# Linear attention: two roundings and the low-rank scaling moved to ScalarE, the low-rank product split over two row groups

## The reference, cut to what matters

```python
def _L0_attn_ref(x, W_q, W_k, W_v, W_g, W_o, log_decay):   # chunks of 32 tokens
    Q = x @ W_q.T; K = x @ W_k.T; V = x @ W_v.T
    S = jnp.einsum('bncd,bnkd->bnck', Qc, Kc) * mask       # mask: decay ** distance, causal
    O = jnp.einsum('bnck,bnkd->bncd', S, Vc).reshape(B, T, D)
    gate = jax.nn.sigmoid(x @ W_g.T)
    return gate * O @ W_o.T + x
def _L0_ffn_ref(x, fast_b, w_fc, w_proj, u, v, gate):
    h = _bitlinear(x, w_fc) + gate * (x @ v.T @ fast_b.T @ u.T)
    r = jnp.maximum(h, 0.0)
    return _bitlinear(r * r, w_proj)
x = _layernorm(x + _L0_attn_ref(x, ...))
x = _layernorm(x + _L0_xattn_ref(x, ctx_1024, ...))
x = _layernorm(x + _L0_ffn_ref(x, ...))
```

## Time and profile before

| | |
|---|---|
| runs | 1279.95, 1280.46, 1281.04 us |
| median | 1280.46 us |
| the profiled execution's own time | 1279.73 us |
| its span in the trace | 1277.7 us |
| granted TensorE clock, mean | 0.999 of full speed |
| linear attention in the trace | from 0 to about 146 us on TensorE |
| PE, DVE, ACT, POOL busy | 98%, 72%, 62%, 60% of the span |

### The profile page before, as it was taken

The page is one execution under the profiler, slowest core; times in us unless marked ns, Lnnn a source line. Parts: engine busy times, 40 slices in busy tenths (PEclk is TensorE's granted clock), DMA queues, the critical chain, the costliest instruction groups (busy, mean ns, idle before and its releaser), DMA issues.

```text
span 1277.7 us, 21198 instructions
## 1 busy us (share of the span) xinstructions
PE 1256.6 (98%) x6900; PEld 844.6 (66%) x6900; DVE 922.2 (72%) x1816; ACT 794.0 (62%) x1061; POOL 768.3 (60%) x445
## 2 busy tenths in 40 slices
PE   8999999999999999999999999999999999999996
PEld 6887856666666666656665666657566655677775
DVE  6888877656775767477577756784766777778887
ACT  3444457655665656566656655574656676788885
POOL 2532368967876679487768767794877687100000
PEclk9999999999999999999999999999999999999999
DMA  6311220001100110010011001100200110021101
GB/s 221 116 67 50 69 66 18 4 1 34 37 2 17 33 19 0 17 50 2 0 33 35 0 17 33 19 0 17 50 2 0 34 18 17 14 70 50 49 17 50
DMA packets 99391, 43.08 MB, mean 34 GB/s; under 512 B 77168, under 2 KB 82048, under 8 KB 99344
## 3 DMA queue, kind: packets, MB, share of 16 engines
q1 hardware_dynamic: 98528, 39.33, 12.4%
q0 software_dynamic: 816, 3.15, 0.7%
HBM read 29.59 MB, written 12.58 MB: 33 GB/s over the span
## 4 chain that ended last, share of the span: by engine, by line
PE 92%; DVE 3%; POOL 2%; issue 1%; ACT 1%; DMA 1%; SPq 0%; POOLq 0%; DVEq 0%
PE ps L1400 17%; PE ps L1375 15%; PE ps L48 12%; PE ps L50 11%; PE ps L49 11%; PE ps L1391 4%; PE ps L1379 4%; PE ps L1436 2%; PE ps L1435 2%; PE ps L1437 2%; PE ps L1412 2%; PE ps L1829 2%; PE ps L1830 2%; PE ps L747 1%; PE ps L57 1%
## 5 line engine op out<-in xcount | busy, mean ns | idle before, releaser
L1200 DVE CUSTOM_DVE_ANT_0 junk<-ps,mask 128x512 bf16<-128x512 f32 x504 | 315.0, 687 | 87.7 <-PE ps L1391 86.3
L1066 ACT ACTIVATE prob<-ps,mcol 128x1024 f32<-128x1024 f32 x256 | 282.2, 1117 | 128.9 <-PE ps L1379 124.0
L981 POOL TENSOR_TENSOR acc<-acc,prob 128x1024 f32<-128x1024 f32 x126 | 300.6, 2385 | 11.5 <-POOL acc L981 0.4
L978 POOL TENSOR_TENSOR acc<-prob 128x1024 f32<-128x1024 f32 x63 | 150.6, 2391 | 193.9 <-ACT prob L1066 192.9
L1400 PE MATMUL ps<-prob,v_b 128*64 128x512 f32 x1024 | 244.5, 598 | 0.0
L995 POOL TENSOR_TENSOR acc_lo<-acc,acc_hi 128x1024 f16<-128x1024 f32 x63 | 136.5, 2167 | 5.1
L1400 PEld LDWEIGHTS ps<-prob,v_b 128*64 128x64 f32 x1024 | 67.8, 136 | 107.4 <-issue 73.7
L1375 PE MATMUL ps<-q_hi,k_hi 64*128 64x512 f32 x512 | 114.3, 442 | 1.8 <-issue 0.7
L1379 PE MATMUL ps<-shift,ones_r 64*128 64x512 f32 x512 | 101.8, 392 | 0.1
L1375 PE MATMUL ps<-q_hi,k_lo 64*128 64x512 f32 x512 | 101.4, 391 | 0.0
L1375 PE MATMUL ps<-q_lo,k_hi 64*128 64x512 f32 x512 | 101.4, 390 | 0.0
(11 more groups left out here) (265 smaller groups left out, 2927.6 us busy)
## 6 DMA issues: line engine op xcount, KB each, us to landing
shift<-nmx SPq DMA_DIRECT2D x512, 0.5 KB, 2.0
x_in<-in_xT SPq DMA_DIRECT2D x8, 512.0 KB, 3.7
x_scratch<-x_a SPq DMA_DIRECT2D x8, 512.0 KB, 2.9
raw<-in_cT SPq DMA_DIRECT2D x8, 512.0 KB, 3.7
raw<-x_scratch SPq DMA_DIRECT2D x8, 512.0 KB, 3.9
y<-x_scratch SPq DMA_DIRECT2D x8, 512.0 KB, 3.7
y_scratch<-y SPq DMA_DIRECT2D x8, 512.0 KB, 2.8
outT<-x SPq DMA_DIRECT2D x7, 512.0 KB, 2.8
```

The costliest lines, as they stand in the source:

```text
L978: pool.tensor_tensor(total, prob[:, 0], prob[:, 1], ALU.add).then_inc(acc_out, 1)
L981: pool.tensor_tensor(total, total, prob[:, kt], ALU.add).then_inc(acc_out, 1)
L1066: act.activation(prob[:, i].rearrange("p h t -> p (h t)"), SCORE[i % 2].rearrange("p h t -> p (h t)"), ACT.Exp, scale=SCALE, bias=mcol[:, ...
L1200: dve.tensor_tensor_reduce(junk[:, t % 2, h], SMAX[t % 2][:, h], mask[:], -1.0, -LOWEST, ALU.add, ALU.min, nmx[:, p % 2, t, h:h + 1]).then ...
```

## The change

- The rounding of `x` for batches 2 to 7 goes from VectorE to ScalarE: `round_x(b+1)` stands in step b between `deviation(b-2)` and `values(b)`; that of batch 2 stands ahead of `values(1)`. It waits for the load of `x`. VectorE waits for it ahead of the subtraction.
- The rounding of the gated product for batches 1 to 7 goes to ScalarE too: `round_gated(b)` behind `square(b-1)`.
- The low-rank scaling (`low_rank(0)` and `low_rank(1)`) goes to ScalarE behind `round_gated(3)` and `round_gated(4)`, and GpSimd's last instruction of each group waits for it.
- ScalarE's hardware loop over pairs of batches is written out; one load of the sigmoid table falls away by that (batch 2).
- `uT` and `mid` are held twice, in partitions 0 to 15 and 64 to 79, by a second DMA of `uT` and a second matmul and copy of `mid`. The two matmuls of `low_rank` take one row group each.

```diff
@@ linear_attention_phase @@
-    uT = sb(ctx, "uT", [RANK, HID], F32)
+    uT = sb(ctx, "uT", [P, HID], F32)
...
-    mid = sb(ctx, "mid", [RANK, D], F32)
+    mid = sb(ctx, "mid", [P, D], F32)
...
+    RANK_ROWS = (slice(0, RANK), slice(DH, DH + RANK))
@@ sync @@
-        sp.dma_start(uT[:], a["uT"]).then_inc(f_in, 16)
+        for rows in RANK_ROWS:
+            sp.dma_start(uT[rows], a["uT"]).then_inc(f_in, 16)
@@ gpsimd @@
             pool.wait_ge(f_step, n + 2)
+            pool.wait_ge(f_low, k + 1)
             pool.tensor_tensor(c["wfc"][:, k], c["wfc"][:, k], wfc[:, k], ALU.add).then_inc(f_step, 1)
@@ scalar @@
+        def round_x(b):
+            act.wait_ge(x_in[b % 2], 8 * (b - b % 2) + 16)
+            act.wait_ge(qm_ps, 2 * b - 2)
+            act.activation(x_hi[:, b % 2], x[:, b % 2], ACT.Copy).then_inc(x_rounded, 1)
+
+        def round_gated(b):
+            act.wait_ge(gate_used, b + 1)
+            act.wait_ge(y_ps, 2 * b)
+            act.activation(og_hi[:], og[:], ACT.Copy).then_inc(og_rounded, 1)
+
+        def low_rank(k):
+            act.wait_ge(f_low_ps, k + 1)
+            act.activation(c["wfc"][:, k, :], VY.rearrange("p a n -> p (a n)"), ACT.Identity,
+                           scale=gt[:, 0:1]).then_inc(f_low, 1)
...
-        act.wait_ge(f_in, 96)
+        act.wait_ge(f_in, 112)
...
+        round_x(2)
         values(1)
         square(0)
-        with act.Fori(2, B - 1, 2) as i:
-            for b in (i, i + 1):
-                front(b)
-                query_copies(b)
-                deviation(b - 2)
-                values(b)
-                square(b - 1)
+        round_gated(1)
+        for b in range(2, B):
+            front(b)
+            query_copies(b)
+            deviation(b - 2)
+            if b < B - 1:
+                round_x(b + 1)
+            values(b)
+            square(b - 1)
+            round_gated(b)
+            if b in (3, 4):
+                low_rank(b - 3)
@@ vector, split_x @@
-            if not (isinstance(b, int) and b < 2):
-                dve.wait_ge(qm_ps, 2 * b - 2)
-            dve.tensor_copy(x_hi[:, par], x[:, par]).then_inc(x_split, 1)
-            dve.wait_ge(x_split, 2 * b + 1)
...
+            if b < 2:
+                dve.tensor_copy(x_hi[:, par], x[:, par]).then_inc(x_split, 1)
+                dve.wait_ge(x_split, 2 * b + 1)
+            else:
+                dve.wait_ge(x_rounded, b - 1)
...
@@ vector, split_gated @@
-            dve.wait_ge(gate_used, b + 1)
-            if b > 0:
-                dve.wait_ge(y_ps, 2 * b)
-            dve.tensor_copy(og_hi[:], og[:]).then_inc(og_split, 1)
-            dve.wait_ge(og_split, 2 * b + 1)
...
+                dve.wait_ge(og_rounded, b)
...
-        def low_rank(k):
-            dve.wait_ge(f_low_ps, k + 1)
-            dve.tensor_scalar(c["wfc"][:, k, :], VY.rearrange("p a n -> p (a n)"), gt[:, 0:1], None,
-                              ALU.mult).then_inc(f_low, 1)
...
-        dve.tensor_copy(mid[:], ST[0:RANK, 0:D]).then_inc(f_mid, 1)
+        for rows in RANK_ROWS:
+            dve.tensor_copy(mid[rows], ST[rows, 0:D]).then_inc(f_mid, 1)
@@ tensor @@
-            pe.wait_ge(f_in, 96)
-            pe.matmul(ST[0:RANK, 0:D], bT[:], vr[:], start=True, stop=True).then_inc(f_mid_ps, 1)
+            pe.wait_ge(f_in, 112)
+            for rows in RANK_ROWS:
+                mm = pe.matmul(ST[rows, 0:D], bT[:], vr[:], start=True, stop=True)
+            mm.then_inc(f_mid_ps, 1)
...
-                mm = pe.matmul(VY[:, n], mid[:, k * P:(k + 1) * P], uT[:, n * T:(n + 1) * T], start=True, stop=True)
+                mm = pe.matmul(VY[:, n], mid[RANK_ROWS[n], k * P:(k + 1) * P], uT[RANK_ROWS[n], n * T:(n + 1) * T],
+                               start=True, stop=True)
```

More of the change, by code:

```diff
@@ L339, in linear_attention_phase @@
     f_above, f_below, f_step = sem("f_above"), sem("f_below"), sem("f_step")
+    x_rounded, og_rounded = sem("x_rounded"), sem("og_rounded")
     STAGED, CHUNKS = ("Wq", "Wk", "Wv"), 2 * DK
+    RANK_ROWS = (slice(0, RANK), slice(DH, DH + RANK))
     QO, G, VY, S, ST = ps[:, 0:2, :], ps[:, 2:4, :], ps[:, 4:6, :], ps[:, 6, :], ps[:, 7, :]
@@ L498, in split_x @@
             dve.wait_ge(x_in[par], 8 * (b - par) + 16)
-            if not (isinstance(b, int) and b < 2):
-                dve.wait_ge(qm_ps, 2 * b - 2)
-            dve.tensor_copy(x_hi[:, par], x[:, par]).then_inc(x_split, 1)
-            dve.wait_ge(x_split, 2 * b + 1)
-            dve.tensor_tensor(x_lo[:, par], x[:, par], f32(x_hi[:, par]), ALU.subtract).then_inc(x_split, 1)
+            if b < 2:
[3 more added lines that the diff above has]
+                dve.wait_ge(x_rounded, b - 1)
+            dve.tensor_tensor(x_lo[:, par], x[:, par], f32(x_hi[:, par]), ALU.subtract).then_inc(
+                x_split, 1 if b < 2 else 2)
         def split_weight(i, w, src):
@@ L594, in split_gated @@
         def split_gated(b):
-            dve.wait_ge(gate_used, b + 1)
-            if b > 0:
-                dve.wait_ge(y_ps, 2 * b)
-            dve.tensor_copy(og_hi[:], og[:]).then_inc(og_split, 1)
-            dve.wait_ge(og_split, 2 * b + 1)
-            dve.tensor_tensor(og_lo[:], og[:], f32(og_hi[:]), ALU.subtract).then_inc(og_split, 1)
+            if b == 0:
+                dve.wait_ge(gate_used, 1)
+                dve.tensor_copy(og_hi[:], og[:]).then_inc(og_split, 1)
+                dve.wait_ge(og_split, 1)
+            else:
+                dve.wait_ge(og_rounded, b)
+            dve.tensor_tensor(og_lo[:], og[:], f32(og_hi[:]), ALU.subtract).then_inc(og_split, 1 if b == 0 else 2)
         def scales():
@@ L648, in step @@
             if b in (3, 4):
-                low_rank(b - 3)
-            if b in (3, 4):
                 compare_in(b - 3)
@@ L784, in step @@
             if b == 1:
-                pe.wait_ge(f_mid, 1)
+                pe.wait_ge(f_mid, 2)
             mean(b - 1)
```

## The result

| | before | after |
|---|---|---|
| median of 5 runs each, run side by side | 1280.49 us (1279.95 to 1282.57) | 1287.77 us (1283.67 to 1288.09) |
| ratio, 95% interval | | 1.0040 (1.0026 to 1.0055) |
| the profiled execution | 1279.73 us, span 1277.7 | 1283.67 us, span 1281.7 |
| ACT, DVE, POOL busy | 62%, 72%, 60% | 63%, 71%, 60% |

The change makes the kernel slower by 0.4%. Measured again, 12 runs beside 35, the same pair gave 1284.73 against 1280.26 us, a ratio of 1.0041 (1.0021 to 1.0061), so the loss is about 4.5 us there. The time after lies above the predicted range, 1278.6 to 1283.3 us.

The account below looks back on a forecast made before the run. The prediction took TensorE, with 92% of the span, as the bound. Its terms, 0.2 + 3.25 - 2.0 - 0.95 = +0.5 us, made 1279.7 into 1280.2; median forecast 1281.0 us, range 1278.6 to 1283.3.

Parts of the forecast that it names:

- What bounds the kernel: Whole kernel: 92% of the span lies on TensorE, so only its own stream or its waits pay.
- The start, +0.2: Start, at middle: second uT load and second small matmul cost about 0.1 us each; bounds 0 and 0.7.
- Rounding of x, +3.25: Linear attention, steps 1, 2, 3, 4 and 6: attend waits 0.65 us each for ScalarE's rounding and value copy.
- Low-rank product, -2.0: Steps 3 and 4: two fp32 matmuls in two row groups take 0.91 us, not 1.91; 1.0 saved, twice.
- Rival B: Low-rank matmul pairs run one after the other, no overlap: +2.0 us, 1283.0; chance 0.10.
- Gated product and scaling at nothing: Linear attention: moving both to ScalarE costs nothing by itself; outputs and scores still find their inputs ready.
- Step 5, -0.95: Step 5: TensorE's stalls from VectorE held by GpSimd at tile_sum shrink from 2.5 to 1.55 us; bounds 0 and -1.85.
- Chances: Whole kernel: forecast 0.70; against a 0.2% difference, faster by more 0.09, slower by more 0.15, within 0.76.
- C: Rival: ScalarE takes x's landing later than thought, 1.1 us a step in place of 0.65: 1284.2 us; chance 0.11.
- The sum: Whole kernel: +0.5 us, made in linear attention and passed on whole; median forecast 1281.0 us.
- W: Theory of the experiments, not the prediction's: x's rounding stands ahead of the value copies, and attend waits for it.

Follow-up runs that it names:

- half of `x` ahead: Kernel before with only x's rounding on ScalarE, 512 columns ahead of the value copies, the rest between them: 1284.35 against 1281.19 us, ratio 1.0024.
- all ahead: Kernel before with only x's rounding moved to ScalarE, ahead of both value copies: 1285.60 against 1280.95 us, ratio 1.0033.
- between: Kernel before with only x's rounding moved to ScalarE, between the two value copies: 1280.30 us, ratio 0.9990.
- with `x` between and the late load: Changed kernel, x rounded between value copies, second uT load behind other weights: 1278.97 against 1280.95 us with three GpSimd waits, 1277.68 against 1281.19 without.
- GpSimd giving way: Changed kernel with three GpSimd waits until tile_sum of that step is done: 1281.53 against 1280.95 us, ratio 1.0003.
- the best kernel: Changed kernel, x rounded between value copies, second uT load behind all other weights, no GpSimd waits: 1277.68 against 1281.19 us, ratio 0.9974.

## Why the prediction was wrong, point by point

- **What bounds the kernel: right.** All but the +0.53 us at the start is waits on TensorE in linear attention, less the saving of the pairs, and what was passed on whole arrived nearly so (+3.7 us at `variance(6)`, +4.0 in the span).
- **The start, +0.2: nothing in this trace, above its bound in others.** From `attend(0)` to `middle` it is 1.99 us (1.98 before), and the second small matmul costs nothing (22.89 - 22.36 = 0.53 us, 0.54 before). The +0.53 ahead of `attend(0)` isn't this term: VectorE waited for the load of `WgT_l` until 7.35 us (6.71 before), and the loads of `uT` are issued only from 12.01. In the profiles of the other kernels `attend(0)` starts anywhere from 19.95 to 22.66 us. In four of the six traces with the second load early `middle` waited 0.86 to 1.04 us for the gate's load, more than the 0.7 of the bound; without it none of eight did.
- **Rounding of x, +3.25: right, and slightly low.** Issue to `attend` was forecast at 5.25 us and measured 5.26, 5.47, 5.45 and 5.39 in steps 1, 2, 3 and 6. Steps 1 to 3 lost 0.68, 0.80 and 0.89 in place of 0.65. In step 4 the wait was covered by the one at `mean`; I had counted it there.
- **Low-rank product, -2.0: right in kind, 15% too large.** The pair takes 1.06 us, so 0.85 is saved, twice: -1.7. Rival B (no overlap) fell.
- **Gated product and scaling at nothing: right for ScalarE, wrong for the rest.** ScalarE reaches the query copies later and no `scores` waits. Timeline of ScalarE, changed kernel, the scaling and what follows it:

```profile
78.90 1.10 ACT L485 ACTIVATE wfc<-ps,gt 128x1024 f32<-128x1024 f32 x1
80.02 1.28 ACT L440 ACT_TABLE_LOAD   x1
81.32 1.03 ACT L440 ACTIVATE gate<-ps 128x1024 f32<-128x1024 f32 x1
```

  0.02 us lies on either side of the table load: the drain that the Trainium skill, "ScalarE: Activation LUTs" (What ACT_TABLE_LOAD costs), adds isn't seen here. But the scaling left VectorE, and the comparison and GpSimd's three instructions behind it moved. Step 4 of the kernel before, VectorE and GpSimd:

```profile
85.68 0.85 DVE L548 TENSOR_TENSOR tile_sum_a<-y_a 128x512 f32<-128x512 f32 x1
```

```profile
81.36 2.16 POOL L414 TENSOR_TENSOR wfc_raw<-above,wfc_raw 128x1024 f32<-128x1024 bf16 x1 [14.45 <-DVE wfc_raw L619]
...
86.06 2.71 POOL L418 TENSOR_TENSOR wfc<-wfc,wfc_raw 128x1024 f32<-128x1024 f32 x1
```

  There `tile_sum` came 0.38 us ahead of L418. In the changed kernel GpSimd's three started 82.87 - 77.63 = 5.24 us after the `gates`, where it had been 5.79 (81.36 - 75.57), while `tile_sum` stayed (10.15 us after, 10.11 before). I had worked out this shift for step 5 and never asked what it does in step 4. It made `tile_sum` the second to come, by 0.20 us; the run with the scaling alone shows the same turn. That is the step that failed: the prediction let VectorE's meeting with GpSimd count in step 5 and nowhere else. -0.35 was forecast for step 4 and +0.51 measured; 0.15 of the 0.86 between them is the low-rank pair, 0.71 the collision.
- **Step 5, -0.95: right.** `tile_sum` was held, as forecast, `mean` waited 1.19 us, and the wait for `x_lo` in step 6 is gone. (The working has small slips, on which nothing hangs: 107.35 should be 107.33 us and 107.55 should be 107.6, and under "Chances" C and half of B make 0.16.) Steps 5 and 6 together were forecast at -1.3 and gave -1.31.
- **The sum: wrong where it passed linear attention's end.** This is the same failed step once more: I took it that nothing outside step 5 collides. Step 7 and the end gave +0.28 and +1.31 us, because a meeting that VectorE had won by 0.05 us was lost by 0.17. Six of the fourteen profiles of this study have this wait of 1.06 us at `variance(6)`, the other eight, before among them, don't. Such a near tie had to be in the range. With step 4 it makes 2.45 of the 3.2 us missing in the trace at `variance(6)`; the +0.53 ahead of `attend(0)` and 0.2 in steps 1 to 3 are the rest.
- **The rivals.** C named ScalarE's hand-over and a figure, 1284.2 us, that happens to lie near the profiled run; its mechanism is only a small part of it. I had no rival for a collision at another place, which was the cause. The Trainium skill, "SBUF — State Buffer" (Who interferes with whom), states the lock that GpSimd and VectorE share; the rows agree with it at each place (2.72, 2.84, 2.75 and 2.77 us for what takes 0.69 or 1.2). I applied it to one place only.
- **Open.** The profiled execution was the fastest of its five; the trace explains 4.0 of the 7.3 us between the two medians there. In the second measurement the medians are 4.5 us apart. What the executions above the profiled one lose more no profile shows. A part goes with the granted clock: of the kernel before, the 24 of 104 executions with a mean of 0.995 or less have medians 1.0, 2.0 and 1.5 us above the others on the three chips, and each of the twelve kernels run beside it has the same sign (1.3 to 5.4 us). Row groups alone had 7 such executions of 12, where the kernel before had 3 of 35 on that chip; the other five have a median of 1280.24 against 1280.08 us, so its +1.6 is mostly this. With the same division half of `x` ahead loses 2.6 us, all ahead 3.7 and between -0.2, which is the order that W expects. The division was made afterwards and leaves executions at 0.996 and above unexplained (1291.21 us for the changed kernel). That the meetings, the wait at `middle` and the landing of `x` (see the end) fall differently from one execution to the next would fit, but wasn't shown.

## What to carry to other kernels

In an engine that works in order, an instruction that waits for a transfer belongs behind everything that the bottleneck needs next: the same rounding costs 4.6 us ahead of two copies and nothing between them, as long as the load lands in its usual 3.3 to 3.8 us. In the one trace of the kernels with `x` between in which it landed after 6.5 us, the second half of `attend` waited 2.43 us for it. Work taken off one engine moves every instruction behind it on every other engine, so list all places where VectorE and GpSimd read SBUF within a microsecond of each other, not only the one where they collide now, and give each near tie a chance and a price (here 0.7 us in step 4 and 1.6 in step 7 and the end). When such a tie matters, a wait that makes GpSimd second can give it back (3.0 us in the trace of the changed kernel), if something that nobody waits for can take the collision. It is no sure gain: with `x` between and the late load the ratio was 0.9981 with these waits and 0.9974 without.

## What the hardware showed beyond expectation

- Two fp32 matmuls over 16 rows (four records) in two row groups take 1.06 us from the first to the next matmul, against 1.91 in one row group. A second small matmul in another column group of the array takes no time that shows (0.53 against 0.54 us).
- The collision costs by who comes first: 0.05 us ahead, `tile_sum` takes 0.69 us; 0.17 us behind, 2.75.
- TensorE's granted clock was at its lower level in one short stretch of the feed-forward block in some executions. Columns: busy us and count by engine, then granted clock, DMA share, GB/s; first GpSimd giving way, then the changed kernel:

```profile
1100.00:1105.00 5.00, 4.80 (x15) 3.61 (x16) 2.74 (x5) 4.90 (x9) 0.00 (x0) 0.66 0.00 0
```

```profile
1100.00:1105.00 5.00, 3.50 (x16) 2.52 (x17) 3.15 (x4) 4.90 (x9) 0.00 (x0) 1.00 0.01 3
```

  0.66 is a mean over 1.2 and 2.4 GHz. The rest of the span behind `variance(6)` was 1130.2 to 1131.0 us in the five kernels with such a stretch and 1128.0 to 1129.0 in the others. So some 1 to 3 us in a single profile go with it; the five have no edit in common.
- One load of `x` landed late. In the best kernel's trace (an execution of 1280.27 us, 2.6 above its median) it was issued at 49.73 us and landed 6.5 us after, where the loads of the changed kernel land in 3.5 to 3.8 from 30 us on. SyncE and GpSimd issuing loads, then ScalarE and TensorE:

```profile
49.73 0.38 SPq L377 DMA_DIRECT2D x_in<-in_xT  x1
```

```profile
49.20 0.74 POOL L405 DMA_DIRECT2D raw<-in_Wv  x1 [0.30 <-POOL wk_lo L411]
```

```profile
56.22 1.06 ACT L479 ACTIVATE x_hi<-x_in 128x1024 fp32r<-128x1024 f32 x1 [3.38 <-DMA x_in<-in_xT]
```

```profile
57.81 1.16 PE L769 MATMUL ps<-s_masked,v_tok 128*128 128x128 f32 x8 [2.43 <-ACT v_tok L461]
```

  GpSimd's load of 1024 KB was issued 0.53 us ahead of it. The scaling alone is the only other trace with that order in step 2 (by 0.98 us), and `x` landed after 5.6 us there; in the other twelve `x` was issued first, by 0.23 us or more, and landed in 3.3 to 3.8 us. So this is a near tie too, and its margin in the changed kernel is 0.28 us. No experiment moved it by itself.
